# Bringing operand stacks through DRAM: 48 runs of 4096 bytes read back, and twelve spills of one product row each

## The chip, the core and the metric

The kernel runs on one core of a Trainium2 chip. TensorE (PE) does the matmuls, VectorE (DVE), ScalarE (ACT) and GpSimd (POOL) the elementwise work, and SyncE (SP) issues nearly all of the DMAs, which run on the core's 16 DMA engines. Each engine takes its own instructions in order, and they wait for each other through semaphores. The metric is the device time of one execution in microseconds.

## The reference

Eight sequences pass through two layers. The first is a cross-attention with 16 heads of 8 channels over 256 positions, followed by a feed-forward; the second is a recurrent time mix with token shift, a scan and a channel mix. Only the scores of the first layer are touched by the change:

```python
q = jnp.transpose(zt_prev + pos_enc(C, Tq, zt_prev.dtype)[None], (0, 2, 1))
kv = jnp.transpose(za + pos_enc(C, Tk, za.dtype)[None], (0, 2, 1))
q = layer_norm(q, ln_q_g, ln_q_b)
kv = layer_norm(kv, ln_kv_g, ln_kv_b)
...
Q = split(q @ Wq)
K = split(kv @ Wk)
V = split(kv @ Wv)
attn = jnp.einsum('bhqd,bhkd->bhqk', Q, K) / math.sqrt(DH)
ctx = jnp.einsum('bhqk,bhkd->bhqd', jax.nn.softmax(attn, axis=-1), V)
ctx = jnp.transpose(ctx, (0, 2, 1, 3)).reshape(B, Tq, C)
y = ctx @ Wo
r = y + q
```

## The kernel before

One batch is one sequence. A table `AT` gives each step of each engine a time, and the next batch does the same 730 ticks later, so several batches are in flight and each engine's instructions of different batches are interleaved in a fixed order. The stages are: the a-stage (layer norm, Q, K, V), the top stage (first pass of the scores, to find each row's maximum), the guard (the maximum turned into rows of the operand), the h-stage (scores again, exponentials, sums, feed-forward), and then the recurrent layer.

A head has only 8 channels, and the kernel computes scores in bf16 with the fp32 operands split into three bf16 parts (`parts[:, 0]` high, `parts[:, 1]` middle, `parts[:, 2]` the rest; last axis is q or k, then 256 positions). For one head the matmul contracts 48 rows: six products of parts (`PRODUCTS` = 6) by 8 channels (`D0`). `Q_ROWS` and `K_ROWS` say which part stands in which of the six product rows: the high part in three of them, the middle part in two, the rest in one. Even heads stand on partitions 0 to 47 of `q_stack` and `k_stack`, odd heads on partitions 64 to 111, and along the free axis are 8 heads by 256 positions in bf16, 4096 bytes.

That rearrangement of channels into rows goes through a DRAM tensor, `stacks`. Per batch SP issues (in this order): six spills at L308, two for each part as ACT and DVE finish it (wait on `s_high`, `s_middle`, `s_parts`); the two loads of a later batch, `xin`, at L299 and L300; and after all spills have landed (L315, wait on `s_spilled`), four reads at L318, for q even, q odd, k even, k odd. PE waits for all four (`s_stacked`) ahead of the first matmul of the top stage, L412. It is in-order, so all that stands behind that matmul on PE waits as well: other heads of the top stage, the h-stage scores (L434) of the batch before, `maa1` (L501) of the recurrent layer. In some batches SP also issues the store `out` (L340) between the spills and the reads. The next a-stage on PE follows the guard matmul of the batch before it.

Of the kernel before, what the change touches and what calls it, by code (L numbers as in the profile page):

```python
# [8 lines left out]
BF16 = mybir.dt.bfloat16  # L9
# [4 lines left out]
B, C, T = 8, 128, 256  # L14
H0, D0 = 16, 8
# [8 lines left out]
PRODUCTS = 6  # L24
# [76 lines left out]
def due(at, engine, op, i=None):  # L101

    offset = AT[engine][op]
    n, rest = divmod(at - (offset if i is None else offset[i]), PERIOD)
    return BATCHES[n] if rest == 0 and 0 <= n < B else None
# [8 lines left out]
def build(nc, x, ctx_in, weights, vecs, pos, first, out):  # L114
    with ExitStack() as stack:
        def sb(name, shape, dt=F32):
            return stack.enter_context(nc.sbuf_tensor(name, shape, dt))
# [11 lines left out]
        def two_sems(name):  # L129
            return [sem(f"{name}{p}") for p in range(2)]  # L130
# [20 lines left out]
        def s0(batch):  # L151
# [13 lines left out]
        parts = sb("parts", [128, 3, 2, T], BF16)  # L165
# [71 lines left out]
        yo = two("yo", [128, E])  # L237


        stacks = nc.dram_tensor("stacks", (2, 2, C, PRODUCTS, T), BF16, kind="Internal").ap()  # L240
        values = nc.dram_tensor("values", (2, 2, 128, NT), F32, kind="Internal").ap()


# [9 lines left out]
        s_x_in, s_spilled, s_stacked, s_guard_in, s_v_out, s_stored = (  # L253
            two_sems(n) for n in ("s_x_in", "s_spilled", "s_stacked", "s_guard_in", "s_v_out", "s_stored"))
# [25 lines left out]
        def dma(batch, count=1):  # L280

            return batch.k * (16 * count) + 16 * count
# [6 lines left out]
        def _(sp):  # L289
# [5 lines left out]
            for at in ticks():  # L295
# [7 lines left out]
                for part in range(3):  # L303
                    if a := due(at, "SP", "spill", part):
                        sp.wait_ge((s_high, s_middle, s_parts)[part], a.n + 1)
                        for side, which in enumerate((Q_ROWS, K_ROWS)):
                            rows = which[part]
                            sp.dma_start(stacks[a.p, side, :, rows, :], parts[:, part, side, None, :].broadcast_to([128, len(range(PRODUCTS)[rows]), T])  # L308
                                         ).then_inc(s_spilled[a.p], 16)
                if a := due(at, "SP", "stack"):  # L310
                    if a.n == 0:
                        sp.wait_ge(s_setup, SETUP)
                    if a.n >= 2:
                        sp.wait_ge(s_score_t, (a.n - 1) * H0)
                    sp.wait_ge(s_spilled[a.p], dma(a, 6))  # L315
                    for side, dst in enumerate((q_stack, k_stack)):
                        for e in range(2):
                            sp.dma_start(dst[a.p][64 * e:64 * e + SCORE_ROWS, :, :],  # L318
                                         stacks[a.p, side].rearrange("(i e d) r t -> e (d r) i t", e=2, d=D0)[e]).then_inc(s_stacked[a.p], 16)
                if g := due(at, "SP", "guard"):  # L320
                    sp.wait_ge(s_guard_c, g.n + 1)
                    for part in range(2):
                        for e in range(2):
                            row = 64 * e + TOP_ROWS + part
# [736 lines left out]
```

## Time and profile before

| what | value |
|---|---|
| median of 3 runs | 508.41 us (506.03 to 513.05) |
| the profiled execution's own time | 510.99 us |
| its span, first to last instruction | 509.2 us |
| PE busy | 393.4 us, 77% |
| DVE, ACT, POOL busy | 296.9, 216.8, 151.9 us |
| mean granted TensorE clock | 0.82 |
| DMA on SP's queue | 35776 packets, 25.86 MB |

The profile is one execution; its span is 1.8 us short of that execution's own time. SPq stands for SP's instruction queue, whose "busy" is the time that it takes to issue a DMA. A DMA's time "to landing" runs from the start of its issue to the last of its semaphore increments. A group of several instructions in a timeline is merged when they follow each other closely.

### The profile page before, as it was taken

What the parts mean: (1) busy time and instruction counts of PE and PEld (TensorE: products, weight loads), DVE (VectorE), ACT (ScalarE), POOL (GpSimd) and SP (SyncE); (2) the same over time, 40 slices, a digit from 0 to 9 for tenths busy, and PEclk for the clock granted to TensorE, in tenths of its full rate; (3) what the DMA queues carried; (4) which work ended last, traced back from release to release, by engine and by line L of the source; (5) the groups of instructions that cost most, each with busy time, mean ns of one, the idle gap of its engine ahead of it and who ended that gap; (6) DMA issues with size and microseconds to landing.
All of it is one profiled execution on the core that took longest, in us unless ns stands there. A gap on an engine that the chain in (4) does not pass through costs nothing.

```text
span 509.2 us, 6723 instructions
## 1 busy us (share of the span) xinstructions
PE 393.4 (77%) x2512; PEld 265.5 (52%) x2512; DVE 296.9 (58%) x626; ACT 216.8 (43%) x473; POOL 151.9 (30%) x104
## 2 busy tenths in 40 slices
PE   1517668859888999699979899998989996685624
PEld 0401423626574768367645665674657564663613
DVE  1126126246565977497859586976786355655611
ACT  0200243563554357336834763476346546124001
POOL 7100100110434052415241813254042407225240
PEclk9999999768966899599859977996897699678555
DMA  8160050060314032403422150305030012003000
GB/s 272 85 144 1 24 122 1 3 144 1 95 52 94 5 92 67 89 12 86 117 40 55 41 135 2 94 14 124 0 95 10 2 44 50 11 3 91 10 1 11
DMA packets 35953, 29.74 MB, mean 58 GB/s; under 512 B 3536, under 2 KB 33616, under 8 KB 35792
## 3 DMA queue, kind: packets, MB, share of 16 engines
q1 hardware_dynamic: 35776, 25.86, 21.0%
q10 hardware_dynamic: 144, 3.45, 1.7%
q8 instruction: 20, 0.33, 0.3%
q14 instruction: 13, 0.11, 0.1%
HBM read 20.78 MB, written 8.39 MB: 57 GB/s over the span
## 4 chain that ended last, share of the span: by engine, by line
PE 38%; DVE 18%; issue 13%; POOL 10%; DMA 9%; ACT 7%; SPq 3%; POOLq 0%; ACTq 0%
DMA k_stack<-stacks 7%; DVE top L809 5%; PE o_bank L550 5%; POOL v_rep L765 4%; PE r_two L501 3%; PE r_one L369 3%; PE h_sum L446 3%; PE o_bank L363 3%; PE r_one L356 3%; PE a_even L412 3%; DVE mixed L872 2%; DVE ruk L888 2%; PE a_odd L389 2%; SPq L318 2%; POOL rstd_a L751 2%
## 5 line engine op out<-in xcount | busy, mean ns | idle before, releaser
L809 DVE TENSOR_REDUCE top<-a_even 128x2 f32<-128x512 f32 x64 | 44.0, 688 | 44.6 <-PE a_even L412 32.6
L626 ACT ACTIVATE probs<-h_even 128x512 f32<-128x512 f32 x64 | 38.4, 599 | 54.6 <-PE h_even L434 29.1
L772 POOL TENSOR_TENSOR hrs<-hvar,mhalf 128x32 f32<-128x32 f32 x8 | 44.4, 5546 | 40.8 <-DVE hvar L929 40.8
L412 PE MATMUL a_even<-k_stack,q_stack 62*128 62x256 bf16 x128 | 31.6, 338 | 30.5 <-DMA k_stack<-stacks 25.7
L809 DVE TENSOR_REDUCE top<-a_odd 128x2 f32<-128x512 f32 x64 | 43.6, 682 | 12.9 <-PE a_odd L412 12.9
L626 ACT ACTIVATE probs<-h_odd 128x512 f32<-128x512 f32 x64 | 38.6, 603 | 17.2 <-PE h_odd L434 16.4
L903 DVE TENSOR_TENSOR_SCAN st<-dec_rep,v_rep 128x1024 f32<-128x1024 f32 x16 | 39.4, 2465 | 10.8 <-ACT dec_rep L697 5.4
L446 PE MATMUL h_sum<-probs,v_pad 128*32 128x256 f32 x512 | 41.8, 455 | 0.0
L765 POOL TENSOR_TENSOR v_rep<-v_rep,rk 128x1016 f32<-128x1016 f32 x16 | 40.1, 2504 | 0.0
L550 PEld LDWEIGHTS o_bank<-W,st 128*128 128x128 f32 x256 | 37.1, 228 | 1.8 <-POOL st L769 1.2
L550 PE MATMUL o_bank<-W,st 128*128 128x16 f32 x256 | 36.7, 288 | 1.1 <-POOL st L769 1.1
L434 PE MATMUL h_even<-q_stack,k_stack 64*128 64x256 bf16 x128 | 31.5, 336 | 5.7 <-ACT probs L626 5.1
L412 PEld LDWEIGHTS a_even<-k_stack,q_stack 62*128 62x128 bf16 x128 | 7.6, 101 | 52.5 <-DMA k_stack<-stacks 29.4
L434 PE MATMUL h_odd<-q_stack,k_stack 64*128 64x256 bf16 x128 | 31.6, 338 | 1.2 <-ACT probs L626 1.1
L412 PE MATMUL a_odd<-k_stack,q_stack 62*128 62x256 bf16 x128 | 30.6, 327 | 2.4 <-DVE top L809 1.8
L775 POOL TENSOR_TENSOR rstd_o<-var_o,mhalf 128x1 f32<-128x1 f32 x8 | 4.4, 551 | 92.0 <-DVE var_o L946 92.0
L751 POOL TENSOR_TENSOR rstd_a<-var_a,mhalf 128x4 f32<-128x4 f32 x8 | 12.0, 1504 | 41.8 <-DVE var_a L795 41.8
L764 POOL COPY v_rep<-initial 128x8 f32<-128x8 f32 x16 | 3.7, 229 | 68.5 <-DMA v_rep<-values 52.1
L446 PEld LDWEIGHTS h_sum<-probs,v_pad 128*32 128x32 f32 x512 | 15.0, 123 | 16.5 <-issue 11.3
L872 DVE SCALAR_TENSOR_TENSOR mixed<-r_one,vec,sx 128x128 f32<-128x128 f32 x48 | 13.8, 343 | 13.4 <-PE r_one L369 13.4
L369 PE MATMUL r_one<-th,W 128*128 128x128 f32 x96 | 21.0, 376 | 0.5 <-ACT th L664 0.5
L769 POOL TENSOR_TENSOR st<-st,rk 128x1024 f32<-128x1024 f32 x8 | 19.0, 2369 | 6.3 <-DVE st L903 6.3
(160 smaller groups left out, 825.9 us busy)
## 6 DMA issues: line engine op xcount, KB each, us to landing
v_rep<-values SPq DMA_DIRECT2D x16, 511.5 KB, 5.4
W<-in_weights ACTq DMA_DIRECT2D x1, 3368.0 KB, 11.1
stacks<-parts SPq DMA_DIRECT2D x16, 192.0 KB, 2.3
q_stack<-stacks SPq DMA_DIRECT2D x16, 192.0 KB, 3.5
k_stack<-stacks SPq DMA_DIRECT2D x16, 192.0 KB, 4.6
stacks<-parts SPq DMA_DIRECT2D x16, 128.0 KB, 1.9
xin<-in_x SPq DMA_DIRECT2D x8, 128.0 KB, 2.2
xin<-in_ctx SPq DMA_DIRECT2D x8, 128.0 KB, 2.3
```

Source lines behind the costliest of these rows:

```text
L369: mm = pe.matmul(dst[:, half * 128:(half + 1) * 128], w(f"maa_w2_{group}", half * 128, 128), th[:, group // 4, :], start=True, stop=True)
L412: mm = pe.matmul(a_score[head % 2][:, j * T:(j + 1) * T], q_stack[g.p][e:e + TOP_ROWS, head // 2, j * 128:(j + 1) * 128], k_stack[g.p][e:e ...
L434: mm = pe.matmul(h_score[head % 2][:, j * T:(j + 1) * T], k_stack[h.p][e:e + GUARD_ROWS, head // 2, j * 128:(j + 1) * 128], q_stack[h.p][e ...
L446: mm = pe.matmul(h_sum[quad * QUAD:(quad + 1) * QUAD, half * T:(half + 1) * T], v_pad[h.p][:, j, HEAD_ORDER[four * 4 + quad], :], probs[(f ...
L550: mm = pe.matmul(o_bank[:, (half * S1 + d) * 16:(half * S1 + d + 1) * 16], st[:, half, d, :], w("heads"), start=True, stop=True)
L626: act.activation(flat(probs[turn % PROBS][:, :, :]), h_score[HEAD_ORDER[turn] % 2][:, :], ACT.Exp, scale=SCORE_SCALE).then_inc(s_probs, 1)
L751: pool.tensor_tensor(rstd_a[:, :], var_a[:, :], mhalf[:, 0:4], ALU.pow).then_inc(s_rstd, 1)
L765: pool.tensor_tensor(kv[:, half, :, 1:NT], v_rep[:, half, :, 1:NT], rk[r.p][:, 1, half, None, 0:NT - 1].broadcast_to([128, S1, NT - 1]), A ...
L772: pool.tensor_tensor(hrs[:, :], hvar[:, :], mhalf[:, :], ALU.pow).then_inc(s_hrs, 1)
L809: dve.tensor_reduce(top[:, :, head], a_score[head % 2][:, :].rearrange("p (a t) -> p a t", a=2), AX.X, ALU.max).then_inc(s_top, 1)
L872: ins = dve.scalar_tensor_tensor(out=mixed[:, group, half, :], in0=src[:, col:col + 128], scalar=v(f"stack{group}_{half}"), in1=sx[:, half ...
L903: dve.tensor_tensor_scan(flat(st[:, half, :, :]), flat(dec_rep[r.p][:, half, :, :]), flat(kv[:, half, :, :]), 0.0, ALU.mult, ALU.add).then ...
```

## The change

The six spills per batch become twelve: one for each of the six product rows of q and of k, each a copy of one part (128 partitions by 512 bytes, 64 KB). Before, one transfer wrote a part into up to three rows by a broadcast source. The tensor in DRAM is laid out anew: even or odd head and channel (16), product row (6), head pair (8), position. With it, for each of the 48 (channel, product row) pairs of one read, the 8 heads by 256 positions are contiguous in DRAM, so that a read has one run of 4096 bytes for each of its 48 partitions, where it had eight runs of 512. For this the columns of `Wq` and `Wk` are permuted on the host, so that Q and K come out with their channels in the order of the DRAM rows. The semaphore wait ahead of the reads counts twelve transfers.

```diff
-        stacks = nc.dram_tensor("stacks", (2, 2, C, PRODUCTS, T), BF16, kind="Internal").ap()
+        stacks = nc.dram_tensor("stacks", (2, 2, 2 * D0, PRODUCTS, H0 // 2, T), BF16, kind="Internal").ap()
...
                         sp.wait_ge((s_high, s_middle, s_parts)[part], a.n + 1)
                         for side, which in enumerate((Q_ROWS, K_ROWS)):
-                            rows = which[part]
-                            sp.dma_start(stacks[a.p, side, :, rows, :], parts[:, part, side, None, :].broadcast_to([128, len(range(PRODUCTS)[rows]), T])
-                                         ).then_inc(s_spilled[a.p], 16)
+                            for row in range(PRODUCTS)[which[part]]:
+                                sp.dma_start(stacks[a.p, side, :, row], parts[:, part, side, :]).then_inc(s_spilled[a.p], 16)
...
-                    sp.wait_ge(s_spilled[a.p], dma(a, 6))
+                    sp.wait_ge(s_spilled[a.p], dma(a, 12))
                     for side, dst in enumerate((q_stack, k_stack)):
                         for e in range(2):
                             sp.dma_start(dst[a.p][64 * e:64 * e + SCORE_ROWS, :, :],
-                                         stacks[a.p, side].rearrange("(i e d) r t -> e (d r) i t", e=2, d=D0)[e]).then_inc(s_stacked[a.p], 16)
+                                         stacks[a.p, side, e * D0:(e + 1) * D0].rearrange("d r i t -> (d r) i t")).then_inc(s_stacked[a.p], 16)
...
-    for n in ("Wq", "Wk", "Wv"):
-        put(n, L0[n])
+    for n in ("Wq", "Wk"):
+        put(n, L0[n].reshape(C, H0 // 2, 2, D0).transpose(0, 2, 3, 1).reshape(C, C))
+    put("Wv", L0["Wv"])
```

The instructions on PE, DVE, ACT and POOL and their order are the same in both kernels; only SP's differ. On SP, in batch 2, this stands in a row in the kernel before (the number behind an x counts instructions; in brackets the semaphores that the first of them waits for):

```order
L308 DMA stacks<-parts 128x3x256 [waits s_a_high]
L308 DMA stacks<-parts 128x3x256
L308 DMA stacks<-parts 128x2x256 [waits s_a_middle]
L308 DMA stacks<-parts 128x2x256
L308 DMA stacks<-parts 128x256 [waits s_a_parts]
L308 DMA stacks<-parts 128x256
L299 DMA xin<-in_x 128x256 [waits s_a_zsum]
L300 DMA xin<-in_ctx 128x256
L318 DMA q_stack<-stacks 48x8x256 [waits s_spilled0,s_h_score_t]
L318 DMA q_stack<-stacks 48x8x256
L318 DMA k_stack<-stacks 48x8x256 x2
```

And this in the changed one, at the same place:

```order
L308 DMA stacks<-parts 16x8x256 [waits s_a_high]
L308 DMA stacks<-parts 16x8x256 x5
L308 DMA stacks<-parts 16x8x256 [waits s_a_middle]
L308 DMA stacks<-parts 16x8x256 x3
L308 DMA stacks<-parts 16x8x256 [waits s_a_parts]
L308 DMA stacks<-parts 16x8x256
L299 DMA xin<-in_x 128x256 [waits s_a_zsum]
L300 DMA xin<-in_ctx 128x256
L317 DMA q_stack<-stacks 48x2048 [waits s_spilled0,s_h_score_t]
L317 DMA q_stack<-stacks 48x2048
L317 DMA k_stack<-stacks 48x2048 x2
```

Six issues have become twelve (six, four and two behind the three waits), everything behind them on SP stands six issues later, and the four reads have kept their place and their waits while the shape of each went from 48x8x256 to 48x2048.

## Rows read from the trace of the kernel before

**Rows 1.** The page: lines of the chain that ended last, shares of the span.
```profile
DMA k_stack<-stacks 7%; DVE top L809 5%; PE o_bank L550 5%; POOL v_rep L765 4%; PE r_two L501 3%; PE r_one L369 3%; PE h_sum L446 3%; PE o_bank L363 3%; PE r_one L356 3%; PE a_even L412 3%; DVE mixed L872 2%; DVE ruk L888 2%; PE a_odd L389 2%; SPq L318 2%; POOL rstd_a L751 2%
```

**Rows 2.** Waits, PE: us in total, times, longest.
```profile
PE a_even L412 <- DMA k_stack<-stacks: 25.7, 8, 10.7
```

**Rows 3.** Timeline, PE: first top matmul of batches 2 and 6 (start, us; idle before).
```profile
111.83 0.39 PE L412 MATMUL a_even<-k_stack,q_stack 62*128 62x256 bf16 x1 [2.31 <-DMA k_stack<-stacks]
...
306.38 0.39 PE L412 MATMUL a_even<-k_stack,q_stack 62*128 62x256 bf16 x1 [0.28 <-DMA k_stack<-stacks]
```

**Rows 4.** Timeline, SP: the six spills of batches 2 to 7 (start, us).
```profile
100.94 3.30 SPq L308 DMA_DIRECT2D stacks<-parts  x6
149.33 3.67 SPq L308 DMA_DIRECT2D stacks<-parts  x6
197.90 4.64 SPq L308 DMA_DIRECT2D stacks<-parts  x6
246.67 3.93 SPq L308 DMA_DIRECT2D stacks<-parts  x6
295.32 4.10 SPq L308 DMA_DIRECT2D stacks<-parts  x6
342.23 3.94 SPq L308 DMA_DIRECT2D stacks<-parts  x6
```

**Rows 5.** Timeline, SP, batch 2: single issues, some left out.
```profile
100.94 0.39 SPq L308 DMA_DIRECT2D stacks<-parts  x1
...
103.27 0.49 SPq L308 DMA_DIRECT2D stacks<-parts  x1
103.80 0.45 SPq L308 DMA_DIRECT2D stacks<-parts  x1
104.28 0.43 SPq L299 DMA_DIRECT2D xin<-in_x  x1
104.76 0.43 SPq L300 DMA_DIRECT2D xin<-in_ctx  x1
105.50 0.33 SPq L318 DMA_DIRECT2D q_stack<-stacks  x1
...
106.90 0.47 SPq L318 DMA_DIRECT2D k_stack<-stacks  x1
```

**Rows 6.** Timeline, SP: the third spill of batches 4 and 6.
```profile
199.43 1.58 SPq L308 DMA_DIRECT2D stacks<-parts  x1
...
296.88 1.01 SPq L308 DMA_DIRECT2D stacks<-parts  x1
```

**Rows 7.** DMAs: the last spill of batch 2 (KB, us to landing).
```profile
stacks<-parts SPq DMA_DIRECT2D x1, 64.0 KB, 1.6
```

**Rows 8.** DMAs: the first and the last of batch 2's four reads.
```profile
q_stack<-stacks SPq DMA_DIRECT2D x1, 192.0 KB, 3.4
...
k_stack<-stacks SPq DMA_DIRECT2D x1, 192.0 KB, 4.9
```

**Rows 9.** DMA engines, 26 to 28 us (spills alone) and 106.5 to 111.2 us (reads).
```profile
DMA packets 1120, 0.54 MB, mean 270 GB/s; under 512 B 64, under 2 KB 1120, under 8 KB 1120
...
DMA packets 1613, 0.79 MB, mean 169 GB/s; under 512 B 72, under 2 KB 1613, under 8 KB 1613
```

**Rows 10.** Timeline, SP: the first two `v_rep` loads, start and us.
```profile
128.98 0.63 SPq L335 DMA_DIRECT2D v_rep<-values  x1
129.65 0.59 SPq L335 DMA_DIRECT2D v_rep<-values  x1
```

**Rows 11.** DMAs: the same two loads (KB, us to landing).
```profile
v_rep<-values SPq DMA_DIRECT2D x1, 511.5 KB, 4.4
v_rep<-values SPq DMA_DIRECT2D x1, 511.5 KB, 6.1
```

**Rows 12.** DMA engines, 7 to 16 us: the large load of the weights.
```profile
DMA packets 133, 3.21 MB, mean 356 GB/s; under 512 B 14, under 2 KB 14, under 8 KB 14
```

**Rows 13.** Windows, behind the wait of batch 2 (PE, PEld, DVE, ACT, POOL, then granted clock).
```profile
111.80:124.00 12.20, 11.52 (x80) 6.92 (x80) 8.62 (x20) 4.21 (x9) 0.00 (x0) 0.74 0.01 1
```

## The prediction

> **What bounds the kernel now.** I read the page's chain first: which line takes the most of it. It is the landing of `k_stack`, 7% of the span [rows 1], some 35 us, so the path through DRAM that the change touches lies on the chain. Next, the waits of PE: the first matmul of the top stage waited for that landing in all 8 batches, 25.7 us together, of which 10.7 in the first batch [rows 2], so 2.1 us on average in the other seven. The timeline gives single waits: 2.31 us in batch 2, only 0.28 us in batch 6 [rows 3]. That difference matters by sign. A landing that comes later moves PE's start by its full amount in every batch. One that comes earlier gains at most the wait that was there.
>
> Is PE's start worth its time? Behind the wait of batch 2, PE was busy 11.52 of 12.20 us and DVE 8.62 [rows 13], because PE's queue holds what piled up behind the waiting matmul. Little of a later start can be made good there. And the next batch's layer norm stands on PE behind this batch's guard, so a delay is handed on to the next batch. I therefore take the change of the landing, summed over eight batches, as the change of the time.
>
> **The path step by step, batch 2.** SP began its six spills at 100.94 us and was done 3.30 us later [rows 4]. The last was issued at 103.80 [rows 5] and landed 1.6 us later [rows 7], at 105.4. Its landing covered both `xin` issues (104.28 to 105.19). The first read was issued at 105.50, the last at 106.90 [rows 5]; they landed at 105.50 + 3.4 = 108.9 and 106.90 + 4.9 = 111.8 [rows 8], and PE started at 111.83 [rows 3]. So 6.3 us from the first read's issue to PE, and 4.6 us from the first spill's issue to the first read's.
>
> **Term 1: twelve spills for six.** What does an issue on SP cost? A transfer of 192 or 128 KB ahead or not, it is nearly the same: 0.49 us for a 64 KB one behind a 128 KB one, 0.45 behind a 64 KB one, 0.43 for `xin`, with a gap of 0.05 us; the two `xin` issues start 0.48 us apart [rows 5]. Those move 128 partitions each, as the new spills do, so I take 0.48 us for each new one. The data is no limit: 64 KB at the 270 GB/s of the spills [rows 9] is 0.24 us, under the spacing. Then twelve take 0.39 + 0.05 + 10 x 0.48 + 0.43 = 5.67 us. After the first issue nothing is waited for on DVE or ACT: six issues of the high part last 2.9 us, and before, the waits for the middle and the last part were over within the 3.30 us that all six needed.
>
> Before, the eight batches took 3 x 3.30 (batches 0 and 1 read as batch 2) + 3.67 + 4.64 + 3.93 + 4.10 + 3.94 = 30.2 us [rows 4]. In batches 4 and 6 one issue was long, 1.58 and 1.01 us [rows 6], against 0.33 to 0.39 for other issues after a pause [rows 5]; I keep those 1.22 and 0.65 us. After: 8 x 5.67 + 1.87 = 47.2 us. The last spill is issued **17.0 us later**, summed over the batches, and it lands as before. The `xin` issues stay hidden under its landing; `out`, where it stands there, too.
>
> Bounds: the longest spacing in the rows is 103.27 to 103.80, 0.53 us, which gives 88 x 0.05 = 4.4 us more, 21.4. The first issues after a pause took 0.33 to 0.39 us; at a spacing of 0.40 it would be 7.0 us less, 10.0. I take 0.48, the row of the same number of partitions and back to back.
>
> **Term 2: reads with runs of 4096 bytes.** From the first landing to the fourth are 2.9 us, 0.97 us for each 192 KB, which is about 200 GB/s; the windows show 169 GB/s with the tail, all packets under 2 KB [rows 9]. The issues are 0.51 us apart, so the transfers, not SP, set this pace. Would longer runs quicken it? Nearest is `v_rep`: 128 partitions by one run of 4092 bytes. The two landed at 128.98 + 4.4 = 133.4 and 129.65 + 6.1 = 135.75 [rows 10, 11], so 2.37 us for 511.5 KB, 221 GB/s. At that pace 192 KB take 0.89 us, 0.08 us less than now: 0.3 us for a batch. Runs eight times as long thus bought hardly anything there. On the other side the spills, with packets of 512 bytes as the reads have, ran at 270 GB/s [rows 9]: the 512 bytes are not what holds the reads at 200. Both say that the pace comes from where the data goes, 48 partitions in each read, and those stay. I take **0.3 us for a batch, 2.4 us in all**.
>
> The Trainium skill has a rule for that, in "SBUF — State Buffer", section "Door 1: The DMA port swizzle": the rate of a DMA depends on how many of the 16 SBUF ports its partitions reach, partitions 0 to 63 reach only eight (about 218 GB/s), and two transfers, one at partition 0 and one at 64, ran only 6% faster together. The trace agrees, with about 200 GB/s for the reads to partitions 0 to 47 and 64 to 111. By that rule the second term is nearly nothing and the forecast stands.
>
> Bounds: at worst nothing is saved (the pace of the 512-byte reads stays). At best the pace is that of the weights' load, which ran at 356 GB/s with long runs [rows 12]: 192 KB in 0.55 us, 4 x 0.42 = 1.7 us a batch, 13.4 us in all. The far end, with no transfer queued behind another, is the last read landing like the last spill, 1.6 us, plus 0.36 us for 128 KB more: 1.40 + 2.0 = 3.4 us to PE where there were 6.3. That would be 2.9 us a batch, 23 us in all.
>
> **What costs nothing.** The permuted weights have the same shape. The `values`, `v_rep` and guard transfers stand behind the reads on SP, and SP comes to them well before their data is ready. The last landing of a batch still is the fourth read.
>
> **The sum.** 17.0 - 2.4 = 14.6 us. The profiled execution took 510.99 us (span 509.2), so this one would take 525.6. The median of the runs is 508.41, 2.6 us lower; on that base the forecast is **523.0 us**, 2.9% slower. About 2% is what a measurement of this kernel can tell from no change.
>
> **Rivals.**
> *The reads do speed up.* If what slows the reads is their addresses in DRAM (512-byte runs 48 KB apart) and not their destination, contiguous runs go at the pace of the weights: 17.0 - 13.4 = 3.6 us, 512.0 us. With term 1 at its low bound it is 10.0 - 13.4 = -3.4 us, 505.0 us. For it: the weights' load comes from DRAM too and has the full rate, and `v_rep` reads each of its runs eight times over, which may cost it something of its own. Against it: 221 GB/s with runs of 4092 bytes. 25%, between 505 and 517 us, all within 2%.
>
> *Faster, on the other side.* New spills issued every 0.40 us (10.0 us) and reads at the far end (-23 us): -13 us. The price per batch is a gain of 1.6 us, which exceeds the old wait of 0.28 us in batch 6, so about 1.3 us are lost there and some in others: -11 us, 497.4 us. It decides for faster as soon as the reads shorten by more than the spills lengthen, over 2.1 us a batch at my spacing. Only an excellent case of both terms gets there: 3%.
>
> *Slower than forecast.* A spacing of 0.53 us (+4.4), and long issues as in batches 4 and 6 in most batches, since twice as many issues can meet one: 0.9 us in four more batches, +3.6. The granted clock may add something: it was 0.74 over the 12.2 us behind the wait [rows 13], part of them at 1.2 GHz, and a longer idle PE may keep it there. The matmuls of the top stage took 0.39 us at that clock; 1 us for a batch would be a lot. Together up to +10 us, 533 us: 12%.
>
> *The change doesn't do what it says.* Were the runs of 4096 bytes still cut into packets of 512 bytes, term 2 would be zero: 525.4 us, inside the forecast's own range.
>
> **How the numbers follow.** Forecast 60%: 517 to 528 us (term 1 between 13 and 20 us, term 2 between 0 and 4). Reads speed up 25%, faster 3%, slower than forecast 12%. The range of 8 in 10 leaves out half of the upper rival and the lower part of the first: 509 to 531 us. Faster by over 2% means under 498.2: 0.03. Slower by over 2% means above 518.6: the upper rival, and all but the lowest tenth or so of the forecast, 0.68. The rest, 0.29, is within 2%.
>
> **What the profile of the changed kernel would show.** Twelve spills merged into one entry of about 5.7 us instead of 3.3 (right) or of 4.8 and less (term 1 too large). In the list of DMAs the four reads landing one after another some 0.9 us apart, the first after over 3 us (right); a last landing of 3 us or less after its issue would mean that contiguous runs are quick. The page's packets under 2 KB should fall by 12288, eight batches of 1536, and larger ones take their place. PE's wait for `k_stack` should grow from 25.7 us to about 40. If that wait grows so and the time doesn't, the step that failed is that PE's start sets the end.

## The result, and the profile after

| | before | changed |
|---|---|---|
| median (lowest to highest), us | 510.73 (506.03 to 514.23), 4 runs | 538.95 (538.49 to 546.12), 4 runs |
| profiled execution, span, us | 510.99, 509.2 | 538.49, 536.7 |
| ratio | | 1.062, 95% interval 1.047 to 1.076 |

The change makes the kernel 6.2% slower. I had forecast 2.9%, 523.0 us, with 531 as the upper end of the range: the sign was right, the size half of it. The median of before came out 2.3 us above the one that I had used.

First the chain that ended last of the changed kernel, by line, and its longest waits of PE; they answer to [rows 1, 2].

```profile
SPq L308 8%; POOL v_rep L764 6%; DMA k_stack<-stacks 5%; DVE top L808 4%; PE h_sum L445 4%; PE o_bank L549 3%; PE r_two L500 3%; PE r_one L368 3%; PE a_even L411 2%; PE r_one L355 2%; PE o_bank L362 2%; DVE mixed L871 2%; POOL rstd_h L753 2%; PE r_two L355 2%; POOL rstd_a L750 2%
```

```profile
PE a_even L411 <- DMA k_stack<-stacks: 56.4, 8, 14.9
```

A line that was not among those listed of the chain before now leads it, with 8% of the span: L308, the issuing of the spills. PE's wait for `k_stack` has grown from 25.7 to 56.4 us, by 30.7; the span grew by 27.5. The prediction had put that wait at about 40 us. So most of the added time went where the prediction looked for it; what the rest of the kernel did meanwhile stands below the table.

Now SP's timeline in the changed kernel, all spills of batches 2 to 7 (they answer to [rows 4]; batches 0 and 1 read 7.70 and 7.63), then some single issues of batch 2 [rows 5], and the PE matmul that it ends in [rows 3].

```profile
110.66 7.63 SPq L308 DMA_DIRECT2D stacks<-parts  x12
163.62 7.65 SPq L308 DMA_DIRECT2D stacks<-parts  x12
215.10 8.72 SPq L308 DMA_DIRECT2D stacks<-parts  x12
266.85 7.64 SPq L308 DMA_DIRECT2D stacks<-parts  x12
319.26 8.90 SPq L308 DMA_DIRECT2D stacks<-parts  x12
373.22 7.64 SPq L308 DMA_DIRECT2D stacks<-parts  x12
...
111.28 0.60 SPq L308 DMA_DIRECT2D stacks<-parts  x1
111.92 0.59 SPq L308 DMA_DIRECT2D stacks<-parts  x1
117.69 0.60 SPq L308 DMA_DIRECT2D stacks<-parts  x1
118.33 0.59 SPq L299 DMA_DIRECT2D xin<-in_x  x1
118.96 0.43 SPq L300 DMA_DIRECT2D xin<-in_ctx  x1
119.79 0.33 SPq L317 DMA_DIRECT2D q_stack<-stacks  x1
...
125.87 0.39 PE L411 MATMUL a_even<-k_stack,q_stack 62*128 62x256 bf16 x1 [6.64 <-DMA k_stack<-stacks]
```

The target of a new spill is cut 16 by 8: its 128 rows of 512 bytes stand in DRAM as 16 groups of 8, with one distance inside a group and another between groups, while its source is 128 partitions. A side is cut as 128 rows when one distance will do for all of them, as on both sides of the old spills. An issue of the new form takes 0.60 us, and the starts of two issues are 0.64 us apart, where I had taken 0.48. Even the first `xin` issue, behind the last spill, takes 0.59, and the second again 0.43: an issue that stands behind a transfer of this form is long too. The twelve last 7.6 us, not 5.7. The DMA list has their landings and those of the first and the last read of batch 2 ([rows 7, 8] before):

```profile
stacks<-parts SPq DMA_DIRECT2D x1, 64.0 KB, 2.0
...
q_stack<-stacks SPq DMA_DIRECT2D x1, 192.0 KB, 3.1
...
k_stack<-stacks SPq DMA_DIRECT2D x1, 192.0 KB, 4.7
```

A spill lands 2.0 us after its issue, not 1.6. The last read was issued at 121.09; first landing 119.79 + 3.1 = 122.9, last 125.8: 0.97 us for each 192 KB, as in batch 2 before. In batch 2 the landings are further apart than in most, though. Over all eight batches the mean spacing of the landings fell from 0.99 to 0.87 us, that is from 199 to 227 GB/s: the runs of 4096 bytes did bring 0.12 us for each 192 KB.

To follow the path in all kernels I cut each batch in two: from the start of the first spill's issue to the start of the first read's (A), and from there to the first top matmul on PE (B). Summed over the eight batches, from each kernel's timeline ("tail" is the stretch from the last batch's first top matmul to the end, with the granted clock in it as a share of full speed):

| kernel | A, us | B, us | A + B against before | span against before | tail, us (clock) | ratio of times (95% interval) |
|---|---|---|---|---|---|---|
| before | 41.3 | 50.2 |  |  | 155.3 (0.73) |  |
| changed | 76.0 | 45.8 | +30.2 | +27.5 | 148.5 (0.79) | 1.062 (1.047 to 1.076) |
| twelve spills, old layout | 57.5 | 50.1 | +16.0 | +28.7 | 162.9 (0.69) | 1.040 (1.030 to 1.051) |
| long runs only | 40.9 | 44.9 | -5.7 | -1.8 | 158.4 (0.72) | 0.989 (0.978 to 1.001) |
| all partitions, short runs | 41.3 | 46.8 | -3.5 | -2.8 | 158.3 (0.72) | 0.995 (0.990 to 1.000) |
| all partitions, long runs, twelve spills | 75.5 | 40.4 | +24.3 | +24.0 | 156.6 (0.73) | 1.047 (1.038 to 1.056) |
| rows outside, all partitions | 40.3 | 55.4 | +4.1 | +0.6 | 152.6 (0.76) | 1.010 (1.002 to 1.018) |
| rows outside, 48 partitions | 40.7 | 58.5 | +7.7 | +10.6 | 157.1 (0.73) | 1.026 (1.019 to 1.033) |
| rows outside, two halves | 40.7 | 38.5 | -12.3 | -11.6 | 156.7 (0.73) | 0.957 (0.947 to 0.968) |
| short runs, two halves | 40.5 | 34.1 | -16.9 | -23.8 | 153.9 (0.74) | 0.957 (0.949 to 0.965) |
| short runs, quarter first | 41.4 | 29.5 | -20.6 | -27.5 | 148.3 (0.78) | 0.962 (0.954 to 0.969) |

All columns but the last come from the one profiled execution of each kernel, which for the twelve spills, the long runs only and both kernels with two halves was in the slower state of this chip, while the ratios compare fast executions alone and the medians below take all.

Of the changed kernel's 30.2 us, A is +34.6 and B is -4.4. The span grew by 27.5 us, and that nearness is in part luck. Between PE's start in one batch and the first spill of the next, batches 0 to 6 took 4.1 us more than before in sum, and the tail took 6.8 us less: 30.2 + 4.1 - 6.8 = 27.5. The tail holds the same instructions in every kernel. Before and changed:

```profile
353.89:509.20 155.31, 111.39 (x666) 82.81 (x666) 85.26 (x185) 52.36 (x117) 49.75 (x27) 0.73 0.10 27
388.21:536.70 148.49, 103.25 (x666) 75.83 (x666) 84.03 (x185) 52.40 (x117) 49.34 (x26) 0.79 0.11 28
```

PE was busy 8.1 us less for the same 666 matmuls, at a granted clock of 0.79 in place of 0.73. Over all eleven kernels the tail goes from 148.3 us to 162.9 us as its clock goes from 0.78 or 0.79 down to 0.69. So a single span can differ by several us for the clock alone, and the phases A and B are the better witness of the change.

### The profile page after: what moved, and what is told of

It reads as the page before. It is cut to its first block, busy times and chain, and to the rows that moved or that the text cites. A ratio compares the mean times of both kernels' runs of the same rounds, so it can differ in the third digit from the quotient of the medians.

```text
span 536.7 us, 6771 instructions
## 1 busy us (share of the span) xinstructions
PE 387.5 (72%) x2512; PEld 258.9 (48%) x2512; DVE 293.4 (55%) x626; ACT 216.9 (40%) x473; POOL 157.0 (29%) x104
## 2 busy tenths in 40 slices
DMA packets 25970, 29.75 MB, mean 55 GB/s; under 512 B 4304, under 2 KB 22096, under 8 KB 25808
## 4 chain that ended last, share of the span: by engine, by line
PE 34%; issue 20%; POOL 13%; DVE 12%; SPq 9%; DMA 6%; ACT 6%; POOLq 0%; ACTq 0%
SPq L308 8%; POOL v_rep L764 6%; DMA k_stack<-stacks 5%; DVE top L808 4%; PE h_sum L445 4%; PE o_bank L549 3%; PE r_two L500 3%; PE r_one L368 3%; PE a_even L411 2%; PE r_one L355 2%; PE o_bank L362 2%; DVE mixed L871 2%; POOL rstd_h L753 2%; PE r_two L355 2%; POOL rstd_a L750 2%
## 5 line engine op out<-in xcount | busy, mean ns | idle before, releaser
L411 PE MATMUL a_even<-k_stack,q_stack 62*128 62x256 bf16 x128 | 32.0, 342 | 61.0 <-DMA k_stack<-stacks 56.4
L625 ACT ACTIVATE probs<-h_even 128x512 f32<-128x512 f32 x64 | 38.4, 599 | 54.7 <-PE h_even L433 30.2
L902 DVE TENSOR_TENSOR_SCAN st<-dec_rep,v_rep 128x1024 f32<-128x1024 f32 x16 | 40.4, 2522 | 11.4 <-ACT dec_rep L696 5.7
L445 PE MATMUL h_sum<-probs,v_pad 128*32 128x256 f32 x512 | 43.2, 468 | 0.0
L549 PEld LDWEIGHTS o_bank<-W,st 128*128 128x128 f32 x256 | 34.8, 216 | 1.8 <-POOL st L768 1.2
L549 PE MATMUL o_bank<-W,st 128*128 128x16 f32 x256 | 34.3, 278 | 1.1 <-POOL st L768 1.1
L750 POOL TENSOR_TENSOR rstd_a<-var_a,mhalf 128x4 f32<-128x4 f32 x8 | 13.9, 1737 | 46.1 <-DVE var_a L794 46.1
L753 POOL TENSOR_TENSOR rstd_h<-var_h,mhalf 128x2 f32<-128x2 f32 x8 | 11.6, 1452 | 43.5 <-DVE var_h L829 43.5
L445 PEld LDWEIGHTS h_sum<-probs,v_pad 128*32 128x32 f32 x512 | 15.4, 126 | 17.5 <-issue 12.3
```

The lines of the kernel that those rows point to most:

```text
L411: mm = pe.matmul(a_score[head % 2][:, j * T:(j + 1) * T], q_stack[g.p][e:e + TOP_ROWS, head // 2, j * 128:(j + 1) * 128], k_stack[g.p][e:e ...
L445: mm = pe.matmul(h_sum[quad * QUAD:(quad + 1) * QUAD, half * T:(half + 1) * T], v_pad[h.p][:, j, HEAD_ORDER[four * 4 + quad], :], probs[(f ...
L549: mm = pe.matmul(o_bank[:, (half * S1 + d) * 16:(half * S1 + d + 1) * 16], st[:, half, d, :], w("heads"), start=True, stop=True)
L625: act.activation(flat(probs[turn % PROBS][:, :, :]), h_score[HEAD_ORDER[turn] % 2][:, :], ACT.Exp, scale=SCORE_SCALE).then_inc(s_probs, 1)
L750: pool.tensor_tensor(rstd_a[:, :], var_a[:, :], mhalf[:, 0:4], ALU.pow).then_inc(s_rstd, 1)
L902: dve.tensor_tensor_scan(flat(st[:, half, :, :]), flat(dec_rep[r.p][:, half, :, :]), flat(kv[:, half, :, :]), 0.0, ALU.mult, ALU.add).then ...
```

## The experiments

**Twelve spills, old layout.** The spill part of the change alone; reads and layout as before.

```diff
-                            rows = which[part]
-                            sp.dma_start(stacks[a.p, side, :, rows, :], parts[:, part, side, None, :].broadcast_to([128, len(range(PRODUCTS)[rows]), T])
-                                         ).then_inc(s_spilled[a.p], 16)
+                            for row in range(PRODUCTS)[which[part]]:
+                                sp.dma_start(stacks[a.p, side, :, row], parts[:, part, side, :]).then_inc(s_spilled[a.p], 16)
...
-                    sp.wait_ge(s_spilled[a.p], dma(a, 6))
+                    sp.wait_ge(s_spilled[a.p], dma(a, 12))
```

> The kernel before with one part of the change alone: each product row is spilled by a transfer of its own (twelve of 64 KB, not six), into the old layout of the DRAM tensor, so that the target of each is 128 rows by 512 bytes as its source is; the reads stay as they were. In the changed kernel each of the twelve issues took 0.60 us, spaced 0.64, where I had taken 0.48. Theory 1, it is the shape: a target of 16 by 8 rows against a source of 128 partitions makes an issue dearer. Then the issues here are spaced 0.48 us, the twelve last 5.7 us and the time is 17 us above the kernel before, some 525 to 528 us. Rival, it is the number: any row of more than a few issues in a row costs 0.64 us each. Then the twelve last 7.7 us and the time is 540 us or more, since the reads are the slow ones.

531.93 us beside 512.21 for the kernel before, ratio 1.040. Its SP timeline in batch 2, then one issue of it and its landing:

```profile
107.28 5.56 SPq L308 DMA_DIRECT2D stacks<-parts  x12
...
108.14 0.43 SPq L308 DMA_DIRECT2D stacks<-parts  x1
```

```profile
stacks<-parts SPq DMA_DIRECT2D x1, 64.0 KB, 1.6
```

Twelve issues last 5.56 us at 0.43 us each. So it is the form of the transfer and not the number: with source and target both cut as 128 rows an issue took 0.43 us, with 16 by 8 against 128 it took 0.60, and the landing goes from 1.6 to 2.0 us. Of the 34.6 us that A grew by, 16.2 are from the number of spills and 18.4 from their form. The time rose by some 20 us (1.040, at least 15), above the 525 to 528 us expected. The sum of the phases, 16.0, lies at the low end of the interval. In the profiled execution the span grew by 28.7 us; of the rest, 7.6 us are its tail, at a clock of 0.69.

**Long runs only.** The other part alone. It reads contiguous pieces of the old layout, so the rows in the stacks are not the right ones.

```diff
-                                         stacks[a.p, side].rearrange("(i e d) r t -> e (d r) i t", e=2, d=D0)[e]).then_inc(s_stacked[a.p], 16)
+                                         stacks[a.p, side, 64 * e:64 * e + 64].rearrange("c r t -> (c r t)").rearrange("(p i t) -> p i t", i=8, t=T)).then_inc(s_stacked[a.p], 16)
```

> The kernel before with the other part alone: the six spills stay, and each of the four reads takes a contiguous piece of the DRAM tensor, 48 partitions by one run of 4096 bytes, where it took eight runs of 512. The rows that are read are not the ones that the scores need, so the output is not the reference's; the work is the same. Theory 1, the pace of the reads is set by the 48 partitions that they go to: the reads land 0.85 to 0.95 us apart, the first read to PE's start takes 5.4 to 6.0 us as in the changed kernel (5.4 to 6.1), and the time is 2 to 5 us under the kernel before. Rival, it was the runs in DRAM, and the twelve spills hid that: the reads land 0.6 us apart, 4.5 us to PE's start, and the time is 12 us or more under the kernel before.

507.47 us beside 512.21 for the kernel before, ratio 0.989 (0.978 to 1.001). The interval just includes no change, so the time alone shows nothing; the phases do. B fell from 50.2 to 44.9 us, 5.6 us a batch, as in the changed kernel (5.7). The rival with 4.5 us and 12 us of gain is out. The window of the first batch's reads (us, five engines, granted clock, DMA share, GB/s):

```profile
31.00:34.00 3.00, 0.00 (x0) 0.00 (x0) 0.00 (x0) 0.00 (x0) 0.00 (x0) 0.50 0.93 212
```

212 GB/s into 48 partitions, with runs eight times as long as before; by the spacing of the landings over all batches 230 GB/s, against 199 before. What long runs give, 0.66 us a batch, is twice my 0.3.

**All partitions, short runs.** Eight rows per channel in DRAM, two of them filled once (zero for q, one for k), and one read for each side into all 128 partitions.

```diff
-        stacks = nc.dram_tensor("stacks", (2, 2, C, PRODUCTS, T), BF16, kind="Internal").ap()
+        stacks = nc.dram_tensor("stacks", (2, 2, C, PRODUCTS + 2, T), BF16, kind="Internal").ap()
...
+                    if a.n == 1:
+                        sp.wait_ge(s_setup, SETUP)
+                        for p in range(2):
+                            for side, src in enumerate((q_stack, k_stack)):
+                                sp.dma_start(stacks[p, side, :, PRODUCTS:, :], src[p][:, 0:2, :]).then_inc(s_padded, 16)
...
-                        for e in range(2):
-                            sp.dma_start(dst[a.p][64 * e:64 * e + SCORE_ROWS, :, :],
-                                         stacks[a.p, side].rearrange("(i e d) r t -> e (d r) i t", e=2, d=D0)[e]).then_inc(s_stacked[a.p], 16)
+                        sp.dma_start(dst[a.p][:, :, :], stacks[a.p, side].rearrange("(i x) r t -> (x r) i t", x=16)).then_inc(s_stacked[a.p], 16)
```

> The kernel before with 8 rows for each channel in DRAM, of which two are filled once at the start (zero for q, one for k), so that each side is read by one transfer into all 128 partitions: 256 KB in runs of 512 bytes, two reads for four. A third more bytes, and the runs stay short. Theory 1, the destination sets the pace: packets of 512 bytes go at the 270 GB/s of the spills, the two reads take 2 us of transfer, and the first read to PE's start falls from 6.3 us to 3.6 us; capped by the waits that PE has to lose, 12 to 17 us are gained, 492 to 498 us. Rival, the short runs set the pace (169 to 200 GB/s): 512 KB take 2.6 us or more, 5.0 us to PE at best when the tail is as now, a gain of 0 to 8 us.

508.07 us beside 512.21, ratio 0.995. The gain of 12 to 17 us did not come: the time lies in the rival's range of 0 to 8. The expectation had an error in it: 128 partitions by 4096 bytes are 512 KB a side, not 256 (before it was 384), so the transfers take longer than it said. Whether the rival's cause, short runs, is the right one shows in the pace. Window of the first batch's reads (a packet's whole time counts where it starts, so that a DMA share can pass 1):

```profile
31.50:34.10 2.60, 0.00 (x0) 0.00 (x0) 0.00 (x0) 0.00 (x0) 0.00 (x0) 1.00 1.17 321
```

321 GB/s with runs of 512 bytes, and 311 by the spacing of the landings over all batches. Runs of that size are not what held the reads at 199 GB/s. Nor is it the size of a transfer: the 256 KB reads of the kernel with short runs and two halves, below, land at 293 GB/s. With a third more bytes B is still 0.4 us a batch shorter.

**All partitions, long runs.** The changed kernel with the same padding; each side is one read of 128 partitions by 4096 bytes.

```diff
-                        for e in range(2):
-                            sp.dma_start(dst[a.p][64 * e:64 * e + SCORE_ROWS, :, :],
-                                         stacks[a.p, side, e * D0:(e + 1) * D0].rearrange("d r i t -> (d r) i t")).then_inc(s_stacked[a.p], 16)
+                        sp.dma_start(dst[a.p][:, :, :], stacks[a.p, side].rearrange("x r i t -> (x r) i t")).then_inc(s_stacked[a.p], 16)
```

> The changed kernel (twelve spills) with the same padding, so that each side is read by one transfer of 128 partitions by one run of 4096 bytes. Theory 1: the reads are at their quickest of all kernels, 3.3 us from the first read to PE's start against 5.4 to 6.1 in the changed kernel; about 2.4 us a batch are gained, 517 to 521 us. Beside the kernel with short runs and all partitions it shows what the length of the runs is worth when the destination no longer limits: 0.3 us a batch or less. Rival, the destination is no limit: 5.5 us to PE's start or more, since a third more bytes are read, and 539 us or more.

534.28 us, ratio 1.047. Its two reads in the first batch, from the timeline and the DMA list:

```profile
33.69 0.33 SPq L321 DMA_DIRECT2D q_stack<-stacks  x1
34.06 0.43 SPq L321 DMA_DIRECT2D k_stack<-stacks  x1
```

```profile
q_stack<-stacks SPq DMA_DIRECT2D x1, 512.0 KB, 4.0
...
k_stack<-stacks SPq DMA_DIRECT2D x1, 512.0 KB, 4.8
```

```profile
35.50:37.50 2.00, 0.00 (x0) 0.00 (x0) 0.00 (x0) 0.00 (x0) 0.00 (x0) 1.00 1.00 379
```

They landed at 37.7 and 38.9 us: 512 KB in 1.2 us, and 1.29 us in the mean of all batches, 407 GB/s; the window has 379. That is 1.8 times the pace of the same runs into 48 partitions. B is 5.05 us a batch, above the 3.3 that the wrong size had given, under the 5.7 of the changed kernel. The expected 517 to 521 us were missed by 13 us, and the rival's 539 was not reached. The gain over the changed kernel in B is 5.4 us; in time, 1.062 to 1.047, some 8 us, with intervals that overlap. Long runs do count in reads of all partitions: 1.29 us for 512 KB against 1.69 in the kernel with short runs, both in the mean. I had said 0.3 us a batch or less; it is 0.8 in B.

**Rows outside, all partitions.** If the product row is the outermost axis in DRAM, the 128 channels have one distance between them, so six spills can do it again, and reads still have long runs.

```diff
+        stacks = nc.dram_tensor("stacks", (2, 2, PRODUCTS + 2, 2 * D0, H0 // 2, T), BF16, kind="Internal").ap()
...
+                            sp.dma_start(stacks[a.p, side, rows].rearrange("r x i t -> (x i) r t"),
+                                         parts[:, part, side, None, :].broadcast_to([128, n, T])).then_inc(s_spilled[a.p], 16)
...
+                        sp.dma_start(dst[a.p][:, :, :], stacks[a.p, side].rearrange("r x i t -> x r i t")).then_inc(s_stacked[a.p], 16)
```

> A DRAM layout with the product row outermost, then even or odd head and channel (16), head pair, position. With it a spill has 128 target rows with one distance between them, so that one transfer can again write up to three product rows (six spills of the old shape), and a read still has runs of 4096 bytes; the rows are padded from 6 to 8 and read by one transfer for each side into all 128 partitions. Theory 1 (an issue costs by its shape, a read by the partitions that it reaches): the spills last 3.3 to 4.6 us as in the kernel before (30 us over the batches, against 63.5 in the changed one), the first read to PE's start takes 5.0 us (5.05 in the mean with twelve spills and the same reads, 6.3 before). The sum of both phases is 10 us under that of the kernel before, of which batch 6 can take only 0.3 and others part: 5 to 9 us are gained, 502 to 506 us where the kernel before takes 511. Rival, source and target that are cut in different ways make a transfer dear: 16 by 8 rows against 128 partitions cost 0.13 us in each issue of the spills, and here the reads have that form, so they take 5.8 us or more and nothing is gained.

514.89 us beside 509.48, ratio 1.010 (1.002 to 1.018). The spills did as expected (A 40.3 us). The rival held for the reads: B is 55.4 us. Same bytes, same 128 partitions, same runs as in the kernel above, but the source is cut 16 by 8, and the runs of neighbouring partitions stand 64 KB apart in DRAM instead of side by side. The two issues, the window of the transfers, and the DMA list:

```profile
29.15 0.62 SPq L323 DMA_DIRECT2D q_stack<-stacks  x1
29.82 0.59 SPq L323 DMA_DIRECT2D k_stack<-stacks  x1
```

```profile
31.40:34.60 3.20, 0.00 (x0) 0.00 (x0) 0.00 (x0) 0.00 (x0) 0.00 (x0) 1.00 1.02 251
```

```profile
q_stack<-stacks SPq DMA_DIRECT2D x1, 512.0 KB, 4.8
...
k_stack<-stacks SPq DMA_DIRECT2D x1, 512.0 KB, 6.2
```

Landings at 33.95 and 36.0, 2.05 us for 512 KB, 251 GB/s in the window with all 16 DMA engines busy (share 1.02), against 1.2 us. That is the pace of `v_rep` in the kernel before (221 GB/s, [rows 10, 11]), whose source is cut 16 by 8 too, and it has the same issue time, 0.63 and 0.59. `v_rep` reads each run eight times over from one small piece of DRAM, so its addresses are of another kind; the slow pace that both have goes with the cut. The distance alone was not varied.

**Rows outside, 48 partitions.** The same layout with 6 rows and four reads; the source of each is cut 8 by 6.

```diff
+                                         stacks[a.p, side, :, e * D0:(e + 1) * D0].rearrange("r d i t -> d r i t")).then_inc(s_stacked[a.p], 16)
```

> The same layout without padding: six spills of the old shape, and four reads of 48 partitions by one run of 4096 bytes, whose source is cut as 8 channels by 6 product rows. It asks whether runs of 4096 bytes needed the twelve spills. Theory 1: the destination sets the pace, so that the reads land 0.85 to 1.0 us apart however the source is cut, 5.6 us to PE's start as with runs alone; 505 to 509 us, 2 to 6 us under the kernel before. Rival, the outermost cut of a transfer says on how many of the 16 DMA engines it runs (the Trainium skill has such a rule, in 'DMA: Bandwidth & Descriptors', section 'Why a DMA increments its semaphore by 16 and not by 1'): 8 engines for both halves, 192 KB at 8 times the 25.8 GB/s that one engine showed with runs of 4096 bytes (159 ns each) take 0.95 us, the same pace; but each issue costs more, 0.64 us like that of the guard rows in place of 0.42, so 6.3 us to PE's start and no gain.

522.61 us, ratio 1.026, B 58.5 us, 7.3 a batch. One issue and the window of the first batch's reads:

```profile
30.01 0.66 SPq L319 DMA_DIRECT2D q_stack<-stacks  x1
```

```profile
31.40:35.00 3.60, 0.00 (x0) 0.00 (x0) 0.00 (x0) 0.00 (x0) 0.00 (x0) 1.00 0.48 163
```

The DMA share is 0.48, and in the trace's packet records eight packets of 4096 bytes are under way at a time where the other kernels with long runs and uncut reads have 16: eight engines of 16 were at work, as the rule quoted in the expectation has it. At 163 GB/s and 0.66 us an issue it is the slowest way to read. Theory 1 is out; the rival had the mechanism but gave 6.3 us and no gain, where 7.3 us and a loss of 2.6% were measured. The layout of the changed kernel, in which each read's source is one contiguous piece, thus has a reason; what it saves in the reads is less than it costs in the spills.

The packets also say why 16 engines bring so little into 48 partitions. The median time of one with 4096 bytes was 159 ns here and in the reads of all 128 partitions with long runs, but 256 ns in the changed kernel and 259 with long runs only, where 16 engines write into 48 partitions, and 273 with rows outside and all partitions. With 512 bytes it was 44 ns into 48 partitions before and 27 into 128. So in the slow reads all engines are at work and each packet takes longer; the engines themselves can go faster.

**Two halves, rows outside.** Each read cut by head pairs; the second half has a semaphore of its own, which PE waits for at the ninth head.

```diff
+                    for half in range(2):
+                        pairs = slice(4 * half, 4 * half + 4)
+                        for side, dst in enumerate((q_stack, k_stack)):
+                            sp.dma_start(dst[a.p][:, pairs, :], stacks[a.p, side, :, :, pairs].rearrange("r x i t -> x r i t")
+                                         ).then_inc((s_stacked, s_stacked_late)[half][a.p], 16)
...
+                        if head == 8:
+                            pe.wait_ge(s_stacked_late[g.p], dma(g, 2))
```

> The same, with each read cut in two by head pairs: first pairs 0 to 3 of q and k, then pairs 4 to 7, on a semaphore of their own that PE waits for at the ninth head of the top stage. Theory 1: PE starts after two transfers of 256 KB, 3.9 us after the first read's issue in place of 5.0; the second pair lands 1.3 us later, long before the ninth head. Since PE had 2.1 us to lose in the mean batch of the kernel before and only 0.3 in batch 6, the further gain is 2 to 6 us: 498 to 504 us. Rival, transfers in flight together share the DMA engines so that the first two land when all four do: PE starts 5 us after the first read's issue and the time is that of the uncut reads.

492.61 us beside 509.48, ratio 0.957. B is 4.8 us a batch against 6.9 uncut: the first halves land first, and PE starts on them. The gain, 17 to 27 us, is more than the 12.3 of the phases, and the time is under the 498 to 504 us expected.

**Two halves, short runs.** The same cut on the padded old layout: six spills, runs of 512 bytes, no permuted weights.

> The layout of the kernel before, padded to 8 rows (runs of 512 bytes, source and target both cut as 128 rows, as in the kernel with all partitions), and each read cut in two by head pairs as in the kernel with two halves. It has no permuted weights, six spills and runs of 512 bytes. Theory 1: what counts is when the first two transfers land. Both reads of 512 KB landed 1.65 us apart with this layout and 2.06 with the runs of 4096 bytes cut 16 by 8; halves land 0.83 us apart, against 0.91 with the long runs, so PE starts 4.5 to 4.9 us after the first read's issue as there, and the time is the same within 4 us, 489 to 497 us, 3.5 to 4.5% under the kernel before. Rival, the long runs are what made that kernel quicker: PE starts 5.3 us or later, 500 us or more.

485.41 us beside 507.07, ratio 0.957 (0.949 to 0.965). All six runs (479.5 to 487.7 us) lie at least 13 us under the lowest of the eleven of the kernel before (501.2). It is the best version together with the one above. The percentage is the one expected, the time itself a little under the 489 to 497 us. Batch 2, SP's reads, then PE's first top matmul, then the kernel's wait of PE:

```profile
98.50 0.38 SPq L323 DMA_DIRECT2D q_stack<-stacks  x1
98.92 0.51 SPq L323 DMA_DIRECT2D k_stack<-stacks  x1
99.46 0.51 SPq L323 DMA_DIRECT2D q_stack<-stacks  x1
100.01 0.51 SPq L323 DMA_DIRECT2D k_stack<-stacks  x1
...
102.76 0.39 PE L419 MATMUL a_even<-k_stack,q_stack 62*128 62x256 bf16 x1 [0.29 <-DMA k_stack<-stacks]
```

```profile
PE a_even L419 <- DMA k_stack<-stacks: 10.0, 3, 8.3
```

PE waits for `k_stack` in only 3 of 8 batches, 8.3 of the 10.0 us in the first one; in four of the others it starts 0.4 to 0.6 us after the landing, so there B no longer measures the path through DRAM alone. B is 4.3 us a batch, a little under the 4.5 to 4.9 expected. The rival, that long runs matter, is out for this version.

**A quarter first.** The cut behind the second head pair.

> The same, with the cut behind the second head pair: first 128 KB of q and of k, then 384 KB of each, which PE waits for at its fifth head. Theory 1: the first two land 4.0 us after the first read's issue; the rest lands at 5.9 us, and the first four heads keep PE and DVE for 2.8 us at 0.7 us a head, so the second wait is short or nothing. 0.7 us a batch under the kernel with halves where PE has a wait to lose: 486 to 493 us. Rival, the second part is then late: PE waits at the fifth head and the time is that of the halves or above.

485.98 us beside 507.07, ratio 0.962 (0.954 to 0.969). B falls to 3.7 us a batch, but the time doesn't follow: the wait that was left in the steady batches was already nothing. Theory 1 promised 0.7 us where PE has a wait to lose, and there was none left; the rival's wait at the fifth head is there in batch 0 alone, 0.85 us. It can't be told from the halves.

## Why the prediction missed

**That the path through DRAM sets the time: right.** PE's wait for `k_stack` grew by 30.7 us, A + B by 30.2, the span by 27.5 (with 4.1 us lost and 6.8 won elsewhere). In the table, taking 5.1 us for 1%, the A + B of most kernels lies within the interval of their ratio. Outside are the rows outside with 48 partitions (7.7 us, where the interval begins at 9.7) and the two kernels with halves. What I had argued for losses holds. For gains the cap by PE's wait was right in kind: the quarter's further 3.7 us brought nothing that the medians show.

**Term 1, the twelve spills: mis-sized, and this is the step that failed.** "Those move 128 partitions each, as the new spills do, so I take 0.48 us for each new one." Measured: 0.64, so 63.5 us of issuing over the batches where I had 47.2, and a term of 33.3 us where I had 17.0. The kernel with twelve spills in the old form shows that 0.48 is right for a target cut as 128 rows (its twelve lasted 5.56 us; I had 5.67). What I passed over is the cut of the target, 16 by 8. The row for it was there: `v_rep` is the only transfer of the kernel before whose two sides are cut 16 by 8 and 128, and its issues took 0.63 and 0.59 us [rows 10]. Those two issues start 0.67 us apart; at that spacing twelve take 11 x 0.67 + 0.59 = 8.0 us, term 1 is 8 x 8.0 + 1.9 - 30.2 = 35.7 us and the forecast 541.7 us, a little too much, beside 538.95 measured. I had used that group for its landings and taken the price of an issue from `xin`. "It lands as before" failed too: 2.0 us instead of 1.6, some 2.7 us over the batches. The upper bound of 0.53 us was the longest spacing in a row of spills, all of the old form, so the range could not hold the result.

**Term 2, the reads: right in kind, half of its size, on a wrong witness.** 2.4 us forecast, 4.4 measured (B, 50.2 to 45.8), 5.3 with long runs alone. That 48 partitions a read go with a slow pace is shown: 199 and 230 GB/s into 48 partitions with runs of 512 and 4096 bytes, 311 and 407 into 128. Why they do is not shown by these runs; the number of rows changed with that of the partitions. The length of the runs is not nothing either: it brought some 15% into 48 partitions and 30% into 128. But `v_rep`, which I called the nearest row, goes to 128 partitions. It was slow for its 16 by 8 cut, as the reads with rows outside show, and proved nothing about 48 partitions; the spills at 270 GB/s were the better sign, though they go the other way. The Trainium skill's rule on ports ("SBUF — State Buffer", section "Door 1: The DMA port swizzle") gave the right answer in place of the wrong row; the trace is near its 218 GB/s, with 199 to 230. The 6% that I cited beside it stand in another section of that page, "Can I just issue two DMAs to hit both halves?".

**Rivals.** "The reads do speed up" (25%) and "faster" (3%) are out. "Slower than forecast" (12%) had a long spacing and long issues as its cause; the long spacing was right in kind, but came from the form and not from the number, and was priced at 4.4 us where 16.3 came, so that its upper end, 533 us, was passed as well. Long issues did not multiply: the spills of batches 4 and 6 are 1.1 and 1.3 us longer than the rest, like before. The granted clock, 0.74 behind the wait of batch 2 before [rows 13], was 0.63 in the changed kernel's batch 2:

```profile
125.80:138.00 12.20, 11.73 (x76) 7.75 (x76) 7.68 (x18) 3.19 (x7) 0.00 (x0) 0.63 0.01 1
```

That fits the 4.1 us lost behind PE's starts in batches 0 to 6, which can be more or less than this cost, since other waits lie there too; the tail, where the clock was higher than before, took 6.8 us less. No run changes the clock by itself.

**Packets.** Those under 2 KB fell from 33616 to 22096, by 11520: the 12288 of the reads, less 768 of 4 bytes, 16 for each of the 48 additional spills. The change did what it says.

**Open.** The two kernels with halves gained 17 to 27 us where the phases gave 12.3 and 16.9. In the profiled execution of the first the span agrees with the phases (-11.6 us), at a mean clock of 0.79; what is left over is in its other runs, of which the one with 483.94 us had a clock of 0.87, while runs of the kernel before had 0.77 to 0.85. In the second the profiled span is 6.9 us further down than the phases, at a mean clock of 0.80, under the 0.82 before: 5.6 us of it lie behind PE's starts in batches 0 to 6 and 1.4 in the tail. So a higher clock may be part of the gain, and in that execution is not all of it. This was not tested by itself. Nor was why a 16 by 8 cut costs up to 40% of the pace. An estimate from the port table of the Trainium skill ("SBUF — State Buffer", section "Door 1: The DMA port swizzle"), if each engine took 8 neighbouring partitions, has two engines at each port and half of the ports idle at any time, 218 GB/s; the 221 and 251 GB/s are near it, but no run here shows which engine writes which partition.

## What to carry to other kernels

Price a DMA's issue, landing and pace from a row with the same cut of both sides, not from one of the same size: here 128 against 128 rows cost 0.43 us an issue, 16 by 8 against 128 cost 0.60, and 8 by 6 against 48 cost 0.66 and half of the engines. Reads into 48 partitions ran at 199 GB/s with runs of 512 bytes and at 230 with runs eight times as long; padding to all 128 brought 311 and 407, but a third more bytes to move, so that little of it reached the time (ratio 0.995). And before a transfer is made quicker, look whether its first user needs all of it: cutting the padded reads in two, with a semaphore of its own for the second part, gave 4.3% against the kernel before, some 4% of it from the cut itself (0.995 to 0.957), more than any layout did.

## What the runs showed that I had not expected

- Two reads of 512 KB into all 128 partitions with runs of 4096 bytes: 1.2 us apart when the source is cut as 128 rows, 2.05 us when it is cut 16 by 8 (first batch; 1.29 and 2.09 in the mean).
- An issue of 0.43 us becomes 0.59 when it stands behind a transfer with a 16 by 8 cut: the first `xin` at 118.33 against the second at 118.96.
- A transfer whose source is cut 8 by 6 ran on eight DMA engines (share 0.48) although it had 48 target partitions, and its packets were as quick as any (159 ns for 4096 bytes), where 16 engines into 48 partitions took 256 to 259 ns for each.
- Runs of 512 bytes into 128 partitions read at 321 GB/s, 1.5 times the 212 of runs of 4096 bytes into 48.
- The same instructions at the end of the kernel took 148 us at a granted clock of 0.79 or 0.78 and 163 us at 0.69, a spread half as large as the whole effect of the change.
